# Layer-1 attention: queries and keys projected once and spread through DRAM; fp32 probabilities as weights of nine-column value products

## What is computed

```
def proj(x, w, bb):
    return (jnp.einsum('bsd,ed->bse', x, w) + bb).reshape(b, -1, NUM_HEADS, D_K).transpose(0, 2, 1, 3)
qh = proj(q, wq, bq); kh = proj(k, wk, bk); vh = proj(v, wv, bv)
scores = jnp.einsum('bhqd,bhkd->bhqk', qh, kh) / math.sqrt(D_K)
scores = jnp.where(mask, jnp.float32(-1000000000.0), scores)
probs = jax.nn.softmax(scores, axis=-1)
out = jnp.einsum('bhqk,bhkd->bhqd', probs, vh)
return jnp.einsum('bsd,ed->bse', out, wo) + bo
```

## Time and profile before

| | us |
|---|---|
| median of 3 runs | 798.11 (797.28 to 801.21) |
| span of the profiled execution | 799.2 |
| stage c, first scores to last residual | 369.5 to 635.1 |

### The profile page before, as it was taken

How to read it: one execution, slowest core, us unless ns; L and a number is a source line. 1 busy time by engine, 2 the same in 40 slices (tenths; PEclk the granted TensorE clock), 3 DMA queues, 4 the chain that set the end, 5 groups by cost and what they waited for, 6 DMA issues and landing times.

```text
span 799.2 us, 13367 instructions
## 1 busy us (share of the span) xinstructions
PE 684.9 (86%) x4150; PEld 531.9 (67%) x4150; DVE 632.0 (79%) x1325; ACT 486.1 (61%) x769; POOL 201.4 (25%) x255
## 2 busy tenths in 40 slices
PE   5765754999999999977899889899888559999996
PEld 3654542878777877754667667677666348888884
DVE  3666666879888988885989989997998578888886
ACT  3332230777777777754969778786786325555553
POOL 3443230000000000042536637454374200000000
PEclk8777665999999999997989989997998659999999
DMA  5322000000000000001101011010110000000000
GB/s 163 102 97 90 0 0 0 1 1 1 0 0 0 0 0 0 1 8 33 33 18 33 22 28 26 14 38 12 30 24 9 2 1 0 14 13 13 13 27 26
DMA packets 32676, 17.90 MB, mean 22 GB/s; under 512 B 20481, under 2 KB 31490, under 8 KB 32642
## 3 DMA queue, kind: packets, MB, share of 16 engines
q1 hardware_dynamic: 31490, 16.20, 7.6%
q10 hardware_dynamic: 1152, 1.28, 0.6%
HBM read 10.26 MB, written 2.10 MB: 15 GB/s over the span
## 4 chain that ended last, share of the span: by engine, by line
PE 58%; DVE 26%; issue 7%; ACT 4%; POOL 2%; DMA 1%; DVEq 1%; SPq 1%; ACTq 0%; POOLq 0%
PE psum L376 12%; PE psum L378 11%; PE psum L377 11%; DVE c_mx L1329 4%; DVE c_sm L1335 2%; PE psum L1154 2%; DVE c_pl L1341 2%; DVE xn L305 2%; DVE w_hi L1314 2%; PE psum L1186 2%; PE psum L1183 2%; PE psum L864 2%; DVE stats L286 2%; DVE c_on L1356 2%; PE psum L1493 2%
## 5 line engine op out<-in xcount | busy, mean ns | idle before, releaser
L376 PE MATMUL psum<-xh,w_hi 128*128 (+1 forms) x272 | 114.2, 420 | 1.7 <-DVE d_hr L1581 1.7
L377 PE MATMUL psum<-xl,w_hi 128*128 (+1 forms) x272 | 109.7, 403 | 0.0
L378 PE MATMUL psum<-xh,w_lo 128*128 (+1 forms) x272 | 109.4, 402 | 0.0
L1432 POOL TENSOR_TENSOR c_pl<-c_pt,c_ph 77x512 f16<-77x512 f32 x64 | 74.8, 1169 | 123.7 <-ACT c_ph L1258 123.7
L819 DVE TENSOR_TENSOR b_hl<-b_hs,b_hh 128x1024 fp32r<-128x1024 f32 x64 | 78.2, 1221 | 16.8 <-ACT b_hh L813 16.6
L924 ACT ACTIVATE b_hr<-psum,b1s 128x512 f32<-128x512 f32 x128 | 81.0, 685 | 16.4 <-PE psum L378 16.4
L1154 PE MATMUL psum<-ident,c_pf 128*77 128x128 f32 x512 | 86.3, 294 | 4.7 <-DVE c_pl L1341 1.9
L813 ACT ACTIVATE b_hh<-b_hs 128x1024 fp32r<-128x1024 f32 x64 | 68.0, 1062 | 33.4 <-PE psum L378 33.4
L969 DVE TENSOR_TENSOR b_hs<-b_hr,psum 128x1024 f32<-128x1024 f32 x64 | 77.8, 1215 | 12.6 <-ACT b_hr L924 10.8
L1258 ACT ACTIVATE c_ph<-psum 77x512 f16<-77x512 f32 x128 | 74.5, 592 | 6.3 <-PE psum L1154 5.1
L262 POOL TENSOR_TENSOR spare_q<-half_neg 1x1 f32<-1x1 f32 x54 | 10.0, 186 | 221.4 <-DVE mv L289 221.4
(11 more groups left out here) (213 smaller groups left out, 1645.3 us busy)
## 6 DMA issues: line engine op xcount, KB each, us to landing
c_kb<-w_lo SPq DMA_DIRECT2D x128, 39.0 KB, 2.0
stage<-in_weights SPq DMA_DIRECT2D x8, 600.0 KB, 4.8
x_all<-in_x SPq DMA_DIRECT2D x8, 256.0 KB, 2.8
out_dram<-x_all SPq DMA_DIRECT2D x8, 256.0 KB, 2.3
ctxg<-in_ctxT SPq DMA_DIRECT2D x8, 156.0 KB, 4.1
ctxg<-in_ctxT ACTq DMA_DIRECT2D x8, 156.0 KB, 2.2
wk<-in_wks SPq DMA_DIRECT2D x1, 256.0 KB
w_wq<-in_wq SPq DMA_DIRECT2D x1, 64.0 KB, 1.8
```

The costliest lines, as they stand in the source:

```text
L376: pe.matmul(o, wh, h, start=start, stop=False)
L377: pe.matmul(o, wh, l, start=False, stop=False)
L378: return pe.matmul(o, wl, h, start=False, stop=stop)
L1432: q_.tensor_tensor(pl_[:, q % NC4, :], pt32[:, q // 2 % 2, :], ph[:, q % NC4, :], ALU.subtract).then_inc(lo_done[0], 1)
```

## The change

Queries and keys of a group are now one product each (`NU` is 2). ScalarE writes the high part with the bias added, VectorE the low part, both over 128 partitions. SP stores both parts to DRAM (`q_dram`, `k_dram`) and reads them back to where the score products want them: twelve DMAs for the keys, to a block diagonal that now holds all four sequences of a group (`kb`, one for each parity), and three for the queries. The score product uses 96 rows in place of 128. Transposed probabilities stay fp32 (`pt`), copied by ScalarE alone; values stay fp32 with a one behind each head (`v4`, 9 columns). A value product is one fp32 product for each head; a call of `values` now makes two quarters. The steps `low`, `combine` and `split_values` are gone, and VectorE inverts and divides from PSUM.

```diff
-        NU = 2 * NC4
+        NU = 2
+        VC = DH + 1
+        pt = sb("c_pt", [S2, NC4, HQ * P])
+        v4 = sb("c_v4", [S2, 2, TG, NH, VC])
+        kb0 = sb("c_kb0", [P, NC4, HQ, TG, SK], F32R)
+        kb1 = w_lo[:, s0:s0 + TG * NC4 * GK].rearrange("p (c j b k) -> p c j b k", c=NC4, j=HQ, b=TG)
...
+            def spread_keys(a):
+                p = a.parity
+                before(sp, u_read, NU, a, 0)
+                sp.dma_start(k_dram[p], khl.bitcast(F32)).then_inc(k_spread[p], 16)
...
+                for s, part in enumerate((0, 1, 0)):
+                    for j in range(HQ):
+                        r = 32 * s + DH * j
+                        src = k_dram[p, :, part, :].rearrange("(c j d) k -> j d c k", c=NC4, j=HQ)[j]
+                        sp.dma_start(kb[p][r:r + DH, :, j, :, :].rearrange("d c b k -> d c (b k)").bitcast(F32), src).then_inc(qk_in[p], 16)
...
+                if a:
+                    load_context(a)
+                    spread_keys(a)
+                    place_keys(a)
+                    spread_queries(a)
+                    place_queries(a)
...
-                    ins = pe.matmul(o, qs[:, m.parity, c, b * P:(b + 1) * P],
-                                    kb[:, b % 2, c, :, :].rearrange("p j k -> p (j k)"), start=False, stop=True)
+                    ins = pe.matmul(o, qs[0:KS, m.parity, c, b * P:(b + 1) * P],
+                                    kb[m.parity][0:KS, c, :, b, :], start=False, stop=True)
...
-                    pe.matmul(o, ph[:, q % NC4, j * P:(j + 1) * P], vv, start=True, stop=False)
-                    ins = pe.matmul(o, pl_[:, q % NC4, j * P:(j + 1) * P], vv, start=False, stop=True)
+                for c in (2 * (k % 2), 2 * (k % 2) + 1):
+                    for j in range(HQ):
+                        h = c * HQ + j
+                        ins = pe.matmul(PV[:, h * VC:(h + 1) * VC], pt[:, c, j * P:(j + 1) * P],
+                                        v4[:, g.parity, b, h, :], start=True, stop=True)
...
-                    g, q = lagged(m, t, i - 6)
-                    if g:
-                        values(g, q)
+                    g, q = lagged(m, t, i - 5)
+                    if g and q % 2 == 1:
+                        values(g, q // 2)
...
-                    if a and m and i < NU:
-                        prepare(a, i)
-                    if t and i == 6:
+                    if a and m and i in (0, 3):
+                        prepare(a, i // 3)
+                    if a and m and i == 6:
+                        prepare_values(a)
+                    if t and i == 7:
                         project(t)
...
+                a_.activation(pt[:, q % NC4, :], bank[2 + q % 2][0:S2, :], ACT.Copy).then_inc(pt_done, 1)
...
-                v.tensor_reduce(o10[:], bank[4][:, 0:NH * 3 * VW].rearrange("p (h s d) -> p h d s", h=NH, s=3),
-                                AX.X, ALU.add).then_inc(o_read, 1)
...
-                    if t and i == 7:
+                    if t and i == 8:
                         residual(t)
```

More of the change, by code:

```diff
@@ L55 @@
 TAKEN = -3.0e38
-HALF_RANGE = 10.397207708399179
+KS = 3 * HQ * DH
 class Group:
@@ L1080, in sp_c, with load_context @@
         def sp_c(sp):
-            def place_keys(g, b):
-                for j in range(HQ):
-                    r = slice(4 * DH * j, 4 * DH * (j + 1))
-                    sp.dma_start(kb[r, b % 2, :, j, :].bitcast(F32),
-                                 ks[r, g.parity, :, b, :].bitcast(F32)).then_inc(kb_placed[b % 2], 16)
+            def load_context(a):
+                if a.i is None and a.c < 2:
+                    sp.wait_ge(a_v_ready, NG)
+                before(sp, v_ready, 1, a, 0, 2)
+                sp.dma_start(ctxg[:, a.parity, :], ctxT[:, a.cols(GK)]).then_inc(c_ctx[a.parity], 16)
@@ new lines, in spread_queries, with place_queries @@
+            def spread_queries(a):
+                p = a.parity
+                before(sp, u_read, NU, a, 1)
+                sp.dma_start(q_dram[p], qhl.bitcast(F32)).then_inc(q_spread[p], 16)
+            def place_queries(a):
+                p = a.parity
+                sp.wait_ge(q_spread[p], a.pair(16, 16))
+                if a.i is None and a.c == 0:
+                    sp.wait_ge(xb.used, NG * E)
+                for s, part in enumerate((0, 0, 1)):
+                    src = q_dram[p, :, part, :].rearrange("(c r) t -> r c t", c=NC4)
+                    sp.dma_start(qs[32 * s:32 * s + 32, p, :, :].bitcast(F32), src).then_inc(qk_in[p], 16)
@@ L1279, in step @@
             def step(a, m, t):
-                if a and m:
-                    load_context(a)
                 if t and not m:
@@ L1292, in step @@
                     if g:
-                        high(g, q)
-                    if a and m and i < NU:
-                        prepare(a, i)
-                    if a and m and i == NU:
+                        copy(g, q)
+                    if a and m and i in (1, 4):
+                        prepare(a, i // 3)
+                    if a and m and i == 7:
                         prepare_values(a)
@@ L1379, in step @@
                     if go and qo % NC4 == 0:
-                        combine(go, qo // NC4)
-                    g, q = lagged(m, t, i - 4)
-                    if g and q % 2 == 1:
-                        low(g, q)
-                    if go and qo % NC4 == 0:
                         invert(go, qo // NC4)
@@ L1726 @@
         x=a["x"], ctxT=ctxT.reshape(D, -1), mask=a["mask_SxS2_bk1"], gates=gates, ident_in=np.eye(P, dtype=np.float32),
-        part_in=lows, rank_in=rank, weights=np.concatenate([part[n] for n in WIDTH], 1),
+        rank_in=rank, weights=np.concatenate([part[n] for n in WIDTH], 1),
         wq0=a["L0_xattn_w_q"], wk0=a["L0_xattn_w_k"], wv0T=a["L0_xattn_w_v"].T,
         b1=a["L0_ffn_b1"].reshape(E, HC, P).transpose(2, 0, 1),
-        bqs=columns(a["L1_xattn_bq"]), wks=stack(a["L1_xattn_wk"].T), bks=columns(a["L1_xattn_bk"]),
+        bqs=a["L1_xattn_bq"][:, None], wks=a["L1_xattn_wk"].T, bks=a["L1_xattn_bk"][:, None],
         wvT=a["L1_xattn_wv"].T, bv=a["L1_xattn_bv"][:, None],
```

264 lines of the change are left out of this document (84 added, 180 removed).

## The result

The changed kernel takes 826.49 us (median of 4 runs, 814.15 to 836.74), the kernel before beside it 797.69 (797.15 to 801.21). The ratio is 1.027, with a 95% interval of 1.019 to 1.035: slower by 2.7%, where 861 us (7.9% slower) was forecast. Once more, as a run of its own beside the kernel before, it took 822.56 (815.25 to 834.98, 6 runs) against 797.94: 1.027 (1.021 to 1.033). The changed kernel's executions differ by 2.8%, those of the kernel before by 0.5 to 1.5%, taken beside each run.

What follows compares the result with a forecast made beforehand. TensorE was to replace VectorE as stage c's bound, at a clock of 0.81: start -5, first group +6, six groups +51, last group +10.5, sum +62.5 on the profile's 799.2, 862, given as 861 us; range 806 to 925.

Steps and rivals of the forecast that it cites:

- The bound and the price of a product: Stage c groups: TensorE replaces VectorE as bound at 32.1 us; 64 new value products add 14.2, loads 0.11 us apart.
- The rival in which the load hides: Value products in stage c: nine columns cost two moves at 0.0275 us spacing; about 735 us in all, chance 0.02.
- The issue gaps: Before value products in stage c, TensorE waits for its own issue at 8 places: 1 us added per group.
- The clock: TensorE's granted clock in stage c falls from 0.93 to 0.81, making a group 32.1 / 0.81 + 1 = 40.6 us.
- the clock stays as it is: Rival for stage c: clock holds at 0.93 to 1.00, giving 822 us at 0.93 or 804 at 1.00; chance 0.22.
- faster: Over 0.5% faster, by two cases: TensorE just below the bound (789 us, 0.06) or load hidden (about 735, 0.02).
- the second rival: Stage c's clock mostly stays down: 914 us at stage a's 0.69, 1050 at 0.50 throughout; chance 0.20.
- stage a's 0.69: Average granted clock in stage a, which has products like the new ones; lower end for the 0.81 taken as middle.
- The 804 us that go with the rule: First rival's full-clock end: continuously busy TensorE holds clock 1.00 in stage c's loop, 33.1 us a group, 804 us.
- The ends: Stage c outside its six groups: start 5 us less, first group 6 more, last group 10.5 more.
- Today VectorE hides it: Stage c: VectorE hides clock falls before the change; afterwards each microsecond of TensorE work at the lower level takes two.

Runs made afterwards that it cites:

- experiment 6: Changed kernel with probabilities as fp16 and values as bf16, one part each, so one 16-bit load per value product: 740.32 us, ratio 0.928 to the kernel before.
- experiment 2: Only queries and keys as one product each through DRAM, value path as in the kernel before: 773.4 us, ratio 0.968 to the kernel before.

## Why the prediction was right or wrong

**The bound and the price of a product: right.** "I take 2 x 0.111 = 0.222": measured 0.111 us from load to load, and 0.22 us for a product by adding 4, 8 and 16 of them (32.76, 33.67, 35.45 against 31.89, the last with 28 columns, as no group of 80 products with 9 ran at full clock). The group's 32.1 us at full clock measured 31.9. "78 or 128 columns make no difference" held at 9, 18 and 28 too. VectorE left the path as worked out, only with 18.5 us and not 16.6. The rival in which the load hides (735) fell for fp32. The Trainium skill ("TensorE: Matmul & The Clock Gate", section "Wait — 56ns, not 53.3ns?") puts the least distance between starts at about 25 ns. A product with 128 columns of fp32 weights doesn't come near that, at 222 ns, while experiment 6 reaches it, at 25 ns, and gives that rival's time (740.32).

**The issue gaps: wrong, small.** I added 1 us for each group, for pauses in front of the value products. In the loop after, the loads of these products have no wait for issue at all. That is 6 us.

**The clock: the step that failed.** "Between 0.69 and 0.93 no row is nearer, so I take the middle, 0.81." Measured are 0.96 in one execution and 0.85 in another. I had 45 us for the clock in the loop (6 x (32.1 / 0.81 - 32.1)). Six groups at full clock are 5 x 31.89 + 29.57 = 189.0 us (the last has no next group to prepare; 29.57 is such a group at clock 1.00 in the run with 64 products and 18 columns). So the clock cost 8.1 us in the first profile and 32.5 in the second. Dividing the work by the mean clock was sound (189.0 / 0.96 = 197, 189.0 / 0.85 = 222); the clock put in was not.

Of the 49 us between the forecast sum of +62.5 and the first profile's +13.2, 37 are this term in the loop, 6 the issue gaps and 3.6 the work at full clock, which I had at 6 x 32.1. The rival "the clock stays as it is", at a chance of 0.22, comes nearest, and its clock of 0.93 to 1.00 holds in the first profile. That its 822 us is also the median is partly luck: its loop was 20 us longer than before, and the two profiles have 4.6 and 29. (The chance of "faster" was given as 0.07; its two cases add up to 0.08.)

The worry itself was not idle: with 25% more of these products the loop's clock is 0.63, and even the 914 us of the second rival is passed. The changed kernel stands just ahead of a slope, and no row of the trace of before says so; stage a's 0.69 was taken for a neighbour without knowing on which side of the slope the new loop lies.

By the rule of the Trainium skill ("TensorE: Matmul & The Clock Gate", section "Why this matters for your kernels") a TensorE that is kept continuously busy holds the higher clock. The trace disagrees: it was busy for 54.60 of 54.60 us at clock 0.50. The 804 us that go with the rule were nearer than mine, its reason doesn't hold.

**The ends.** The start gained 3.5 us (I said 5). The wait behind `xl` shrank by 5.0 us, to the 2.7 of the constants, as worked out; but `xl` itself ended 1.6 us later than before, for a reason that is open (it starts at 360.6 to 368.4 in the profiles of the runs). The first group came to +4.3 (I said +6), its clock was 0.81 as assumed. The last came to +6.9 and +3.4 in the two profiles (I said +10.5), at clock 0.71 and 0.78 where I had 0.81 and then half.

**What the whole is made of.** "Today VectorE hides it", I wrote of a fall of the clock, and this is mostly wrong. In the profile of before, these are three groups of the loop, from the first maximum of one to that of the next:

```profile
430.02:461.16 31.14, 27.81 (x284) 20.92 (x281) 28.84 (x57) 25.49 (x45) 17.61 (x23) 1.00 0.12 28
494.92:526.64 31.72, 28.56 (x284) 22.29 (x281) 28.93 (x58) 26.21 (x45) 17.55 (x23) 0.95 0.10 24
526.64:562.10 35.46, 32.45 (x284) 24.14 (x281) 29.42 (x58) 25.52 (x45) 17.53 (x23) 0.86 0.11 23
```

A short fall (0.95) cost 0.6 us then and 1.6 now (33.5 against 31.9, windows between markers). But a longer one (0.86) cost 4.3 then and 4.9 now (36.8 against 31.9), so VectorE hid little of it. At full clock a group took 31.1 us and now takes 31.9. The six groups from 396.25 to 593.23 us took 197.0 us, 10.1 more than 6 x 31.14, so the clock cost the loop before no less than the 8.1 us of the first profile after, and I had set the new group against 32.1 us in which it was already paid. In that profile the loop's 4.6 us more are work, and the rest of the 13 us is the first and the last group, both at a lower clock than before (0.81 against 0.88, 0.71 against 0.75), less the gain at the start. What other executions have on top, up to the medians' 25 to 29 us, is the clock's as far as the second profile shows. The first half of the change takes work from VectorE and TensorE and is worth 25 us by itself (experiment 2); the second spends it on loads, which put TensorE where VectorE had been.

**Open.** Why the low stretches last 10 us in one execution and 55 in another isn't settled, nor what starts the short falls that stay at 28 columns. That the moved columns themselves, and not the other layouts of `v4` and of the result in PSUM that come with them, bring the clock back is the simplest reading; the layouts were not tried apart.

## What to carry to other kernels

Price a product with few moved columns by its weight load, and an fp32 one by two: 0.22 us here for 128 columns of weights, against 0.025 for one 16-bit load. Taking work from one full engine and giving it to another only moves the bound. A loop that fills TensorE pays every fall of the clock, and one that leaves it some slack here was spared part of the short falls only; split such a change and keep the half that pays (here the projected-once queries and keys, 3.2%). Where long loads with few moved columns fill TensorE, vary their number by some per cent before trusting a time: 25% more cost 18% of the time here.

## What the runs showed of the hardware

- The granted clock fell and stayed at its lower level (1.2 GHz) with TensorE busy all the time: 54.60 of 54.60 us.
- Columns that nobody reads, moved under a load that is waited for anyway, made the kernel faster: 970 to 857 us with 80 products, at a loop clock of 0.63 and 0.90. With 64 products a group at full clock took 31.89 us with 9, 18 and 28 columns.
- Loads of 128 columns of weights lay 0.111 us apart in fp32 and in fp32r at clock 1.00 (0.217 in fp32 at 0.50), and 0.025 us apart in fp16. An fp32 product had two of them, an fp32r product one.
- Two executions of one program ran within 0.35 us of each other at each marker up to 545 us and then parted by 20 us in all, with the clock at 0.50 for 10.3 us in one and for 54.6 in the other.
